# A new order for block 1, and the second block's weights rounded in its last steps and in block 2's first

## What is computed

```
x = x + block1(layernorm(x))   # 4 experts, FF 256; a token's id picks its one expert; g = silu(x W^T), u = x W^T, y = (g*u) W, one matrix for all three
x = x + block2(layernorm(x))   # 8 experts, FF 176; the router's two best scores pick and weigh (softmax over the two)
#   y += w_e * W3_e (silu(W1_e x) * (W2_e x))   for every expert e
```

## Time and profile before

| | us |
|---|---|
| median of 3 runs | 177.41 |
| lowest and highest | 175.45, 177.95 |
| the profiled execution | 176.84 |
| its span, first to last instruction | 174.7 |

### The profile page before, as it was taken

One profiled execution on the slowest core, in us unless ns is written; L12 is line 12 of the kernel. 1 busy time (PEld: TensorE's weight loads), 2 busy tenths in 40 slices (PEclk: granted clock), 3 DMA queues, 4 the chain that ended last, 5 costly groups with the idle time before them and its releaser, 6 DMA issues.

```text
span 174.7 us, 2525 instructions
## 1 busy us (share of the span) xinstructions
PE 154.2 (88%) x909; PEld 130.7 (75%) x909; DVE 97.3 (56%) x248; ACT 66.7 (38%) x123; POOL 38.7 (22%) x39
## 2 busy tenths in 40 slices
PE   5964998967878968969999969999999999999991
PEld 1333797946778957748888858988888888888891
DVE  1668346789537625417745945664444744444443
ACT  2360656474694781133222282023222222222220
POOL 0101771764973850027000200000000000000000
PEclk9996599999999999799999999999999999999999
DMA  4992241243282112002100000000000030000003
GB/s 107 281 375 91 53 99 63 43 133 94 66 232 98 60 36 88 0 30 90 30 4 2 0 0 0 4 0 0 0 0 4 3 117 0 0 4 0 2 2 120
DMA packets 5245, 10.18 MB, mean 58 GB/s; under 512 B 913, under 2 KB 2065, under 8 KB 5233
## 3 DMA queue, kind: packets, MB, share of 16 engines
q1 hardware_dynamic: 4560, 8.58, 15.5%
q0 software_dynamic: 528, 1.44, 3.2%
q10 hardware_dynamic: 144, 0.00, 0.0%
HBM read 8.05 MB, written 1.97 MB: 57 GB/s over the span
## 4 chain that ended last, share of the span: by engine, by line
PE 62%; DVE 17%; ACT 10%; issue 6%; another core or an unknown queue 2%; DMA 1%; DVEq 0%; ACTq 0%
PE bank L877 33%; PE bank L893 16%; PE bank L754 3%; DVE hT_lo L594 3%; PE bank L774 2%; DVE act L582 2%; ACT w_hi L373 2%; ACT norm L407 2%; ACT hT_hi L394 2%; PE bank L775 2%; PE bank L776 2%; PE bank L806 1%; DMA ids_sb<-token_ids_dram 1%; DVE stats L611 1%
## 5 line engine op out<-in xcount | busy, mean ns | idle before, releaser
L877 PE MATMUL bank<-hT_hi,w_hi 128*128 128x512 f32 x88 | 35.5, 404 | 1.6 <-DVE gated L731 1.6
L472 ACT ACTIVATE silu<-bank 128x512 f32<-128x512 f32 x22 | 13.2, 599 | 59.7 <-PE bank L877 59.7
L877 PE MATMUL bank<-hT_lo,w_hi 128*128 128x512 f32 x88 | 35.2, 400 | 0.0
L877 PE MATMUL bank<-hT_hi,w_lo 128*128 128x512 f32 x88 | 35.2, 400 | 0.0
L731 DVE TENSOR_TENSOR gated<-gate,bank 128x512 f32<-128x512 f32 x22 | 15.1, 687 | 34.5 <-PE bank L877 28.6
L893 PE MATMUL bank<-w_hi,act_lo 128*128 128x256 f32 x88 | 25.0, 284 | 0.0
L893 PE MATMUL bank<-w_hi,act_hi 128*128 128x256 f32 x88 | 24.8, 282 | 0.0
L893 PE MATMUL bank<-w_lo,act_hi 128*128 128x256 f32 x88 | 24.7, 281 | 0.0
L669 DVE TENSOR_TENSOR act_lo<-act,act_hi 128x512 fp32r<-128x512 f32 x22 | 15.2, 692 | 10.5 <-ACT act_hi L425 10.4
L332 POOL TENSOR_TENSOR w_lo<-raw,w_hi 128x768 fp32r<-128x768 f32 x11 | 20.1, 1836 | 2.9 <-ACT w_hi L373 2.9
L877 PEld LDWEIGHTS bank<-hT_hi,w_hi 128*128 128x128 f32 x88 | 16.9, 193 | 4.9 <-issue 1.8
(11 more groups left out here) (103 smaller groups left out, 240.2 us busy)
## 6 DMA issues: line engine op xcount, KB each, us to landing
raw<-weights_dram SPq DMA_DIRECT2D x11, 384.0 KB, 4.1
raw<-weights_dram SPq DMA_DIRECT2D x4, 256.0 KB, 5.3
out_dram<-x_sb SPq DMA_DIRECT2D x4, 256.0 KB, 2.5
y_rows<-xg SPq DMA_DIRECT2D x3, 256.0 KB, 2.1
x_sb<-x_dram SPq DMA_DIRECT2D x2, 256.0 KB, 4.6
x_sb<-x_dram SPq DMA_DIRECT2D x1, 512.0 KB, 4.5
y_rows<-xg SPq DMA_DIRECT2D x1, 128.0 KB, 1.7
xg<-x_dram,from_x POOLq DMA_INDIRECT x7, 3.1
```

The costliest lines, as they stand in the source:

```text
L472: nc.scalar.activation(silu[:, q % BUFFERS, :], z_of(q)[0][:], ACT.Silu).then_inc(silu_done, 1)
L877: return nc.tensor.matmul(o[:], w[:, c, cols], toks[:, g, k, :], **flags)
```

## The change

- DVE's `var` and `shift` instructions (L560, L565, L616, L621) are gone. POOL's `deviation` and `deviation2` make all four steps: var + eps, -mean, the power, and -mean * rstd, with waits on a semaphore of its own between them.
- The one-hots of the sort (`experts_of_tiles`, `tile_one_hots`, `place_one_hots`) move on DVE from ahead of A0 into A0, behind x_low(1) and weight1_lo(2) and (3). PE's inversion (L924) and its loading of the experts' addresses into registers move from A0 to A1, `sources` (L540) from A0 to A1 behind a_low(0). PE gets 18 instead of 16 warming matmuls at the start, and 6 in A0.
- Statistics of the slot tiles run in A4 to A7 with s-2 instead of A3 to A6 with s-1 (the same sets, one step later), and normalise on ACT stands ahead of silu in A6 to A9 instead of behind the rounding in A4 to A7.
- On PE, down1(s-2) stands ahead of the stages of the step instead of behind them. `transpose_tokens` and the hi and lo parts of the first group move from A12 to A11, `scores`, `best_two` and tanh from A13 to A12.
- The rounding of weight pieces 0 to 4 moves to A9 to A13, that of pieces 5 to 10 to B0 to B5. POOL makes lo parts 0 to 4 behind the last `deviation`, then runs `bring_back`, then lo parts 5 to 10, then the last `deviation2`. SP loads pieces 0 to 4 and x's second half at the start, and pieces 5 to 10 behind the four stores of sorted results.

```diff
-WARM = (4, 16)
+WARM, FILL = (4, 18), 6
...
     "sum": (("A", 6), ("A", NA - 2), ("B", 5)),
-    "shift": (("A", 7), ("A", NA - 1), ("B", 6)),
     "normalise": (("A", 7), ("A", NA - 1), ("B", 6)),
-    "transpose_tokens": (("A", NA), ("B", 7)),
-    "tokens_hi": (("A", NA), ("B", 7)),
-    "tokens_lo": (("A", NA), ("B", 7)),
-    "scores": (("A", NA + 1), ("B", 8)),
-    "best_two": (("A", NA + 1), ("B", 8)),
-    "tanh": (("A", NA + 1), ("B", 8)),
+    "transpose_tokens": (("A", NA - 1), ("B", 7)),
+    "tokens_hi": (("A", NA - 1), ("B", 7)),
+    "tokens_lo": (("A", NA - 1), ("B", 7)),
+    "scores": (("A", NA), ("B", 8)),
+    "best_two": (("A", NA), ("B", 8)),
+    "tanh": (("A", NA), ("B", 8)),
...
-ROUND_AT = {("A", 1 + c): (c,) for c in range(CHUNKS)}
+EARLY = 5
+ROUND_AT = {("A", NA + 2 - EARLY + c): (c,) for c in range(EARLY)} | {("B", c - EARLY): (c,) for c in range(EARLY, CHUNKS)}
...
             sp.dma_start(router_raw[:], router).then_inc(router_in, 16)
-            for c in range(CHUNKS):
+            for c in range(RING):
                 load_w2(c)
             sp.dma_start(x_sb[:, DENSE:, :], x_v[:, DENSE:, :]).then_inc(x_in[2], 16)
             for k in range(NS):
...
+            for c in range(RING, CHUNKS):
+                load_w2(c)
...
             def deviation2(m):
-                pool.wait_ge(var2_done, m + 1)
-                nc.gpsimd.tensor_tensor(rstd2[:, span(SUMS[m])], var2[:, span(SUMS[m])], minus_half[:, 0:len(SUMS[m])], ALU.pow)\
-                    .then_inc(rstd2_done, 1)
+                pool.wait_ge(mean2_done, m + 1)
+                cols = span(SUMS[m])
+                nc.gpsimd.tensor_scalar(var2[:, cols], mv2[:, cols, 1], EPS, None, ALU.add).then_inc(chain, 1)
+                nc.gpsimd.tensor_scalar(minus_mean2[:, cols], mv2[:, cols, 0], -1.0, None, ALU.mult).then_inc(chain, 1)
+                chained[0] += 3
+                pool.wait_ge(chain, chained[0] - 1)
+                nc.gpsimd.tensor_tensor(rstd2[:, cols], var2[:, cols], minus_half[:, 0:len(SUMS[m])], ALU.pow).then_inc(chain, 1)
+                pool.wait_ge(chain, chained[0])
+                nc.gpsimd.tensor_tensor(shift2[:, cols], minus_mean2[:, cols], rstd2[:, cols], ALU.mult).then_inc(shift2_done, 1)
...
             deviation(2)
+            deviation(3)
+            deviation2(0)
+            deviation(4)
+            deviation(5)
             weight_lo(0)
-            deviation(3)
-            weight_lo(1)
-            deviation(4)
-            weight_lo(2)
-            deviation2(0)
-            deviation(5)
-            for c in range(3, 8):
-                weight_lo(c)
             deviation2(1)
-            for c in range(8, CHUNKS):
+            for c in range(1, EARLY):
                 weight_lo(c)
             pool.wait_ge(slot_done, 1)
             pool.wait_ge(y_out, 16 * NS)
             for t in range(SORTED):
                 bring_back(t)
+            for c in range(EARLY, CHUNKS):
+                weight_lo(c)
             deviation2(2)
...
                     take_y(s - 3 - NP)
+                if 6 <= s < 6 + NS:
+                    normalise(s - 3)
...
-                if 4 <= s < 4 + NS:
-                    normalise(s - 1)
...
-            shifts(0)
             weight1_lo(0)
             weight1_lo(1)
             x_low(0)
             slots_of_tokens()
-            experts_of_tiles()
-            tile_one_hots()
-            dve.wait_ge(consts_h_in, 16)
-            place_one_hots()
...
                 if s == 0:
-                    sources()
                     weight1_lo(2)
                     weight1_lo(3)
+                    experts_of_tiles()
+                    tile_one_hots()
+                    dve.wait_ge(consts_h_in, 16)
+                    place_one_hots()
                     statistics(1)
-                    shifts(1)
                 if s == 1:
+                    sources()
...
                 if 4 <= s < 4 + NS:
-                    shifts(s - 2)
-                if 3 <= s < 3 + NS:
-                    statistics(s - 1)
+                    statistics(s - 2)
...
                 if s == 0:
+                    warm(FILL)
+                if s == 1:
                     pe.wait_ge(placed, 1)
...
-                stages("A", s)
                 if s >= 2:
                     down1(s - 2)
+                stages("A", s)
```

More of the change, by code:

```diff
@@ L158, in ffn_moe @@
         minus_half = sb("minus_half", [P, 4])
+        minus_mean = sb("minus_mean", [P, NLN])
+        minus_mean2 = sb("minus_mean2", [P, TILES])
         stats2 = sb("stats2", [P, TILES, 6])
@@ L209, in ffn_moe @@
         xg_in = [sem(f"xg_in{i}") for i in range(N1)]
-        var_done, rstd_done, shift_done, norm_done = sem("var_done"), sem("rstd_done"), sem("shift_done"), sem("norm_done")
+        mean_done, shift_done, norm_done, chain = sem("mean_done"), sem("shift_done"), sem("norm_done"), sem("pool_chain")
         xT_done, g_hi_done, g_lo_done = sem("xT_done"), sem("g_hi_done"), sem("g_lo_done")
@@ L481, in _ @@
         def _(dve):
-            chain = [0]
+            linked = [0]
             def link(ins):
-                chain[0] += 1
+                linked[0] += 1
                 ins.then_inc(vector_chain, 1)
-                dve.wait_ge(vector_chain, chain[0])
+                dve.wait_ge(vector_chain, linked[0])
             def expert_masks():
@@ L548, in statistics @@
             def statistics(n):
-                rows = span(LN_TILES[n])
                 if n < 2:
@@ L558, in statistics @@
                     last = nc.vector.bn_aggr(mv[:, i, :], stats[:, i, :])
-                link(last)
-                nc.vector.tensor_scalar(var[:, rows], mv[:, rows, 1], EPS, None, ALU.add).then_inc(var_done, 1)
-            def shifts(n):
-                dve.wait_ge(rstd_done, n + 1)
-                rows = span(LN_TILES[n])
-                nc.vector.scalar_tensor_tensor(shift[:, rows], mv[:, rows, 0], -1.0, rstd[:, rows],
-                                               ALU.mult, ALU.mult).then_inc(shift_done, 1)
+                last.then_inc(mean_done, 1)
             def x_low(xs):
@@ L614, in sum_and_statistics @@
                     last = nc.vector.bn_aggr(mv2[:, t, :], stats2[:, t, :])
-                link(last)
-                nc.vector.tensor_scalar(var2[:, cols], mv2[:, cols, 1], EPS, None, ALU.add).then_inc(var2_done, 1)
-            def shifts2(m):
-                dve.wait_ge(rstd2_done, m + 1)
-                cols = span(SUMS[m])
-                nc.vector.scalar_tensor_tensor(shift2[:, cols], mv2[:, cols, 0], -1.0, rstd2[:, cols],
-                                               ALU.mult, ALU.mult).then_inc(shift2_done, 1)
+                last.then_inc(mean2_done, 1)
             def tokens_lo(g):
@@ L679, in stages @@
             def stages(kind, i):
-                for m in due("shift", kind, i):
-                    shifts2(m)
                 for g in due("tokens_lo", kind, i):
```

15 lines of the change are left out of this document (10 added, 5 removed).

## The result

| | before | after |
|---|---|---|
| median, us | 176.43 | 180.93 |
| lowest and highest | 175.24, 177.95 | 180.82, 181.38 |
| span of the profiled execution | 174.7 | 179.0 |

The changed kernel is slower: the ratio is 1.029 with a 95% interval of 1.0232 to 1.0348. 173.7 was predicted. The kernel before was measured again beside each set of runs, and its median moved between 173.97 and 176.82, so kernels of different sets are compared by their ratios or by their traces.

What follows compares the result with a forecast made beforehand. PE was taken as the bound, busy 88% of the span, with gains only from block 1's idle time and slow clock. Terms -6.5 - 1.0 + 2.1 + 0.9 + 0.8 = -3.7 gave 173.7 us, range 170.3 to 178.5.

Steps and rivals of the forecast that it cites:

- A4 to A9 (-6.5): Steps A4 to A9 of block 1, 27.95 us: nearly all waits on ACT and DVE lists come back, -6.5 us.
- three causes: In A4 to A9: DVE's shift behind POOL's lo part, normalise waiting for statistics, weight pieces on ACT; 7.1 us together.
- Start (-1.0): Up to up1(4): the clock stays at full pace, less 1 us for loading PE's registers; -1.0 us.
- Tail (+2.1): Block 1's end, from D (start of up1(10)) to B0: two PE holes, 2.3 and 2.7 us; +2.1 us.
- Clock in the tail (+0.9): Block 1's tail: slow clock adds between nothing and twice the earlier loss of 0.9 to 1.6 us; +0.9 us.
- Block 2 (+0.8): Block 2: POOL's last lo part may delay the sums and second norm; ends -0.1 and +1.8, taken +0.8 us.
- Cover: 5 us: Block 2: margin by which late lo parts are ready before PE needs them, 5 us, 1.8 at the least.
- rival C: Clock falls in the tail holes, at the start and behind B7's hole: slower, +1.7, 179.1 us; chance 0.12.
- A: Tail costs little, clock unchanged there, all 7.1 us back, POOL yields to DVE in B5: 171.3 us; chance 0.18.
- B: ACT and DVE go on holding block 1's steps; only 3.5 of 7.1 us back: 176.7 us; chance 0.24.
- D: Block 2: up(5) to up(10) wait for lo parts, 181 us or more; chance 0.05.
- three signs of being wrong: PE idle in A4 to A9 above 3 us; tail and clock over 4.5; any of up(5) to up(10) awaiting lo parts.

Runs made afterwards that it cites:

- fill_tail: The changed kernel with 10 and 12 warm matmuls on PE in the two holes of block 1's tail: 176.36 us against 175.2, ratio 1.0102.
- norm_later: The changed kernel with the second group's sum, norm, transposes, scores and gates one step later: 176.72 us, ratio 1.0033.
- both: The changed kernel with take_y(1) and take_y(2) moved ahead on ACT and the second group's norm one step later: 169.99 us against 174.27.

## Why the prediction was wrong

**A4 to A9 (-6.5): right, -6.07.** PE's idle time there is 0.5 us. The prediction named three causes and gave none its share, so the number doesn't bear out each of them. The two half changes give shares in part: the order alone gives 2.3, the split alone 3.8, and they add up. What the split took away, ACT's pieces or the lo parts on POOL that DVE's shift had met, isn't told apart: it took both out of these steps.

**Start (-1.0): half, -0.47.** The clock stayed at 1.00 behind a hole of 1.79, as forecast. PE's wait at 19.12, where the registers are loaded, is 0.66 us of issue against 1 assumed. The term failed at up1(1): 16.33 where 15.8 was forecast. (The old hole of 2.22 us had little ahead of it, not nothing: PE was busy 0.64 of the 2.46 us from 12.00 to 14.46.)

**Tail (+2.1): right.** Holes 2.25 and 2.65 against 2.3 and 2.7, released by take_y as forecast; with the clock kept, B0 came at D + 16.65 against D + 16.6.

**Clock in the tail (+0.9): mis-sized.** up1(10) to up(2) grew by 4.14, of which the two terms had 3.0. fill_tail puts the slow clock's whole price at 3.5 us; the slow spell ran on from scores through down1(11) into B0, ten microseconds, where the prediction counted only matmuls behind scores and took a value between none and twice the loss of before. By its own figure for that loss, 0.9 to 1.6, the clock took 1.9 to 2.6 more than before: the upper end was the nearer one.

**Block 2 (+0.8): this is the step that failed.** It measured +6.66 (0.39 + 6.11 + 0.16). Three of its links broke.
- "Cover: 5 us" looked only at whether PE waits for a lo part. It never does. But the lo parts held DVE, and the sums stand in DVE's list behind the held operations. Price: all of the 2.06 us by which PE came earlier. The prediction assumed a wait of at most one POOL operation (1.84), from the one coincidence in the earlier trace rows, and priced it only at the sums; the held subtraction took 6.10, and another operation ahead of the sums 2.33.
- The sums: 1.66 longer. That is near the upper end (1.84) of the prediction's range for them, and not the middle that it took. With 0.3 more in the deviation and a start 0.18 later, the norm was 2.13 later. The Trainium skill (GPSIMD Engine Reference, Specifications) says that POOL shares its SBUF interfaces with DVE and collides with DVE instructions that have two SBUF inputs; the trace agrees, with sums of 3.08 us beside a lo part against 1.42 without.
- Only the lateness of the norm was priced, not that PE would be there 2 us sooner. PE's gain turned into a hole, and the hole took the clock with it: 1.9 us, a cost that rival C had at 1.6 for just this place but that the sum left out.

Together that is 2.06 + 2.13 + 1.9 = 6.1 us in this stretch, where 0.8 was forecast.

**The rivals.** C named the mechanism of part of the loss (clock falling in the tail and behind B7's hole, a hole "of 2.5 or more") and gave 179.1; it was thought to decide over 4.6 us lost to the clock. The clock took 1.9 to 2.6 more than before in the tail and 1.9 in B7, 3.8 to 4.5 together, which is less than that. So the nearness of its 179.1 to the measured 180.93 is partly luck: it had 1.4 us for the start, which kept its clock, and only the sum's 0.8 for the 4.2 us by which B7's hole grew. A (the tail's clock unchanged) and B (block 1's steps still held) fell with the clock of 0.50 in the tail and the 0.5 us of idle time in A4 to A9. D (an up waiting for a lo part) didn't happen in any run. No rival said that POOL's row would stall DVE and give back the whole head start; the nearest was one sentence of the block 2 part. Nor did any of the three signs of being wrong show: idle time in A4 to A9 of 0.5 (over 3), tail and clock 4.14 (over 4.5), no up waiting for a lo part. They watched the places that the prediction knew of.

## What to carry to other kernels

When work moves from a stage where an engine is the bound to one where "it has room", count what it does to the engine beside it too: follow each of that engine's lists to the next point where the bound engine waits, not only to the moved work's own consumer. A gain of x us ahead of a join is worth x only if every engine that feeds the join gains x or had that much to spare. And where a neighbour must pass, give the moved work gaps (a wait on the neighbour's progress) and let what feeds the join go first: here this made 1.029 into 0.989. With the tail's take_y moved and the norm a step later it was 0.965; how much of the last step is each repair's isn't told apart.

## What the runs showed of the hardware that was not expected

- A DVE subtraction of 0.69 us took 6.0 to 6.6 us, until 0.55 us behind the end of a row of POOL operations, when it had begun in the last 0.5 us of an indirect DMA on POOL (once 0.02 behind it) that the row followed without a wait. The row's make (3 operations of 1.84, 6 of 1.0, 0.42 and then 3) made no difference. In rows without that start no operation took over 2.4, and with that start but POOL waiting behind the DMA the subtraction took 0.69.
- POOL pays as well: a lo part that DVE's operations meet takes 2.22 to 2.25 instead of 1.84 us.
- Two holes of 2.25 and 2.65 us, with 1.5 us of full work and scores between them, brought 10 us at the 1.2 GHz level; 22 warm matmuls in them kept 2.4 GHz and gave PE 3.5 us back. A hole of 1.79 at the start, with six warm matmuls ahead of it, left the clock at 1.00. Holes in block 2 of 1.83 left it too, and holes of 4.3 to 5.6 didn't. In between it went both ways: behind a hole of 2.64 (norm_later) the clock fell to 0.50 for some 3 us, behind one of 2.63 at the same place of the work (both) it stayed at 1.00. These are their rows:

```profile
105.83 1.19 PE L825 MATMUL bank<-consts_sb,norm 128*128 128x128 f32 x8 [2.64 <-ACT norm L421]
100.73 1.09 PE L829 MATMUL bank<-consts_sb,norm 128*128 128x128 f32 x8 [2.63 <-ACT norm L421]
```

- Small POOL operations (var, -mean, the product) take 0.20 to 0.24 us each for four columns. The power for four columns takes 1.36 in every run where POOL makes all four steps and 1.04 in those where it makes the power alone; why is not shown.
